# Attention score banks of a fused attention and mixture-of-experts kernel: two heads' third key blocks share a bank, and the loop's step is reordered

## What is computed

```
h = xn @ W1 + b1                       # q, k, v of 16 heads, d = 8
w = einsum(q, k) / sqrt(8), causal
a = softmax(w) @ v
attention = a @ Wp + bp
ffn(x) = (silu(x @ gate.T) * (x @ up.T)) @ down.T     # 352 hidden
routed = top-2 of 8 experts by softmax(xn @ gate_w.T), weights renormalised
out = x + attention + shared_ffn(xn) + routed(xn)
```

## Time and profile before

| | |
|---|---|
| Median of 3 runs | 563.29 us (558.61 to 565.58) |
| The profiled execution | 564.77 us |
| Its span, first to last instruction | 563.0 us |
| Mean granted TensorE clock | 0.931 |
| PE, DVE, ACT, POOL busy | 92%, 70%, 55%, 57% |
| Attention loop, about | 16.7 to 333 us of the span |

### The profile page before, as it was taken

How to read it: one execution, slowest core, us unless ns; L and a number is a source line. 1 busy time by engine, 2 the same in 40 slices (tenths; PEclk the granted TensorE clock), 3 DMA queues, 4 the chain that set the end, 5 groups by cost and what they waited for, 6 DMA issues and landing times.

```text
span 563.0 us, 13933 instructions
## 1 busy us (share of the span) xinstructions
PE 519.4 (92%) x4584; PEld 339.4 (60%) x4585; DVE 396.2 (70%) x753; ACT 310.1 (55%) x684; POOL 322.8 (57%) x382
## 2 busy tenths in 40 slices
PE   8879999989999899998988898999999999999995
PEld 3334445444454454444444247999999999977673
DVE  6895678886879878678777555555555555548896
ACT  2015878776777767687666653433333333355542
POOL 5449652342558768577777723676665544475442
PEclk9875999998989999799889669999999999999998
DMA  5424631130111435613111112221122222334555
GB/s 160 153 83 165 209 142 65 48 125 22 59 58 49 168 114 189 184 49 129 36 53 36 49 29 58 62 69 57 58 68 61 56 67 64 113 108 126 156 154 148
DMA packets 52156, 53.46 MB, mean 95 GB/s; under 512 B 5744, under 2 KB 39568, under 8 KB 51856
## 3 DMA queue, kind: packets, MB, share of 16 engines
q1 hardware_dynamic: 47616, 43.71, 24.6%
q0 software_dynamic: 4352, 8.95, 4.8%
q10 hardware_dynamic: 144, 0.20, 0.1%
HBM read 20.38 MB, written 17.90 MB: 68 GB/s over the span
## 4 chain that ended last, share of the span: by engine, by line
PE 68%; DVE 12%; ACT 8%; issue 6%; DMA 4%; DVEq 1%; POOL 1%; SPq 1%; ACTq 0%; POOLq 0%
PE av_bank L879 15%; PE av_bank L1052 9%; PE mx_pair L824 8%; DVE neg_max L1542 5%; PE st_banks L852 5%; ACT probs L1243 4%; PE st_banks L1063 4%; DVE o_sb L1718 3%; PE mx_pair L1038 2%; PE mx_pair L1042 2%; PE mx_pair L1041 2%; PE mx_pair L1043 2%; PE mx_pair L1039 2%; PE mx_pair L1040 2%; PE st_banks L1028 2%
## 5 line engine op out<-in xcount | busy, mean ns | idle before, releaser
L1542 DVE TENSOR_REDUCE neg_max<-mx_pair 128x2 f32<-128x256 f32 (+3 forms) x256 | 203.0, 822 | 64.6 <-PE mx_pair L835 61.9
L1243 ACT ACTIVATE probs<-st_banks 128x512 f32<-128x512 f32 (+1 forms) x384 | 181.3, 526 | 78.9 <-PE st_banks L852 76.6
L852 PE MATMUL st_banks<-q_st,k_st 32*128 32x128 f32 (+3 forms) x512 | 98.6, 414 | 18.2 <-ACT probs L1243 17.2
L705 POOL DMA_INDIRECT y_tok<-y_sb,y_rows x72 | 70.0, 972 | 76.1 <-ACT y_sb L1348 61.5
L824 PEld LDWEIGHTS mx_pair<-k_st,q_st 31*128 31x128 f32 x512 | 45.0, 193 | 96.4 <-DVE neg_max L1542 53.3
L879 PE MATMUL av_bank<-probs,v_wide 128*18 128x512 f32 (+3 forms) x1024 | 100.4, 491 | 0.0
L824 PE MATMUL mx_pair<-k_st,q_st 31*128 31x256 f32 (+3 forms) x512 | 91.7, 399 | 8.8 <-DVE neg_max L1542 8.5
L852 PEld LDWEIGHTS st_banks<-q_st,k_st 32*128 32x128 f32 x512 | 49.4, 193 | 36.1 <-ACT probs L1243 24.3
L629 POOL DMA_INDIRECT sorted_x<-xn_rows,slot_idx x64 | 63.5, 993 | 13.3 <-issue 12.7
L1341 ACT ACTIVATE sg<-mx_pair 128x352 f32<-128x352 f32 x72 | 33.4, 464 | 61.6 <-PE mx_pair L1043 61.6
L588 POOL TENSOR_SCALAR_AFFINE_SELECT probs<-probs 128x1024 f32<-128x1024 f32 x32 | 34.9, 1092 | 53.6 <-ACT probs L1243 53.6
(11 more groups left out here) (214 smaller groups left out, 897.9 us busy)
## 6 DMA issues: line engine op xcount, KB each, us to landing
sorted_x<-zeros SPq DMA_DIRECT2D x8, 580.5 KB, 4.2
xg<-sorted_x SPq DMA_DIRECT2D x36, 129.0 KB, 2.2
picked<-y_tok SPq DMA_DIRECT2D x16, 256.0 KB, 3.8
q_st<-q_hi SPq DMA_DIRECT2D x14, 256.0 KB, 2.5
k_st<-k_hi SPq DMA_DIRECT2D x14, 256.0 KB, 2.5
egu_lo<-in_e_gu SPq DMA_DIRECT2D x2, 1408.0 KB, 6.6
x_all<-in_x SPq DMA_DIRECT2D x8, 256.0 KB, 3.6
att_T<-a_T SPq DMA_DIRECT2D x8, 256.0 KB, 2.1
```

The lines of the kernel that those rows point to most:

```text
L705: pool.indirect_dma_start(y_tok, bass.IndirectOffsetOnAxis(ap=y_rows[:, t, k:k + 1], axis=0), y_sb[t % 2][:, k, :], None).then_inc(y_st[t ...
L852: ins = pe.matmul(st_banks[:, i % 3, lo:lo + w], k_st[buf][32 * j:32 * j + 32, g, kb * P:(kb + 1) * P], q_st[buf][32 * j:32 * j + 32, g, k ...
L1243: act.activation(dst, src, ACT.Exp, scale=SCALE).then_inc(st_free, 1)
L1542: ins = dve.tensor_reduce(neg_max[:, g, h:h + 2, qb], mx_pair[i % 2][:, :, lo:lo + (qb + 1) * P], AX.X, ALU.max, negate=True)
```

## The change

The third key blocks (block 2) of two heads now share one bank: unit 8 holds heads 0 and 1, unit 9 heads 2 and 3, 256 columns for each head. `third_scores(n, 0)` writes the left halves (heads 2 and 0) in visit 4, `third_scores(n, 1)` the right halves (heads 3 and 1) in visit 5, after a wait for the left ones (`third_half`). ACT takes both banks after visit 5, with two exponentials of 512 columns in place of four of 256. On PE, V3 moves to where V1 was, V1 to where V3 and V2 were, and V2 to between visit 4 and visit 5. The second misc work moves behind visit 5, and ACT copies it out after the exponentials of units 9 and 8. ACT's copy of `av_bank` moves behind the exponentials of heads 4, 5 and the first misc work. The new PE order is: visit 0 (S 2, 3), V0, visit 1 (S 0, 1), `m`, V3, visit 2 (S 6, 7), V1, visit 3 (S 4, 5), first misc, visit 4 (left halves), V2, visit 5 (right halves), second misc.

```
-ST_PARTS = [[(0, 0)], [(3, 0), (1, P)], [(2, 0)]]
+ST_PARTS = [[(0, 0)], [(3, 0), (1, P)]]
+THIRD = 8
...
-        scored = [("S", s, u) for u in (2, 3, 0, 1, 6, 7, 4, 5, 10, 11, 8, 9)] if s >= 0 else []
-        order += scored[0:4] + ([("m", s + 1)] if -1 <= s < GROUPS - 1 else []) + scored[4:8] + first_misc(s) + scored[8:10] + second_misc(s) + scored[10:12]
+        scored = [("S", s, u) for u in (2, 3, 0, 1, 6, 7, 4, 5, THIRD + 1, THIRD)] if s >= 0 else []
+        order += scored[0:4] + ([("m", s + 1)] if -1 <= s < GROUPS - 1 else []) + scored[4:8] + first_misc(s) + scored[8:10] + second_misc(s)
...
+            def third_scores(n, k):
+
+                b, g = divmod(n, NG)
+                buf = b % NBUF
+                w = S - 2 * P
+                if k == 1:
+                    pe.wait_ge(third_half, 2 * (n + 1))
+                for half in (1, 0):
+                    i, j = ST_NO["S", n, THIRD + half], 2 * half + k
+                    if k == 0:
+                        pe.wait_ge(st_free, i - 2)
+                    pe.matmul(st_banks[:, i % 3, k * w:(k + 1) * w], k_st[buf][32 * j:32 * j + 32, g, 2 * P:3 * P],
+                              q_st[buf][32 * j:32 * j + 32, g, 2 * P:S], start=True, stop=True,
+                              skip_group_check=True).then_inc((third_half, st_full)[k], 1)
...
-                if kb == 1:
+                if kb in (1, 3):
                     pe.wait_ge(masked, 3 * n + 2)
...
                 if valued:
-                    values(s - 1, 1)
+                    values(s - 1, 3)
                 if maxima:
                     max_scores(s + 2, 2)
...
                 if valued:
-                    values(s - 1, 3)
-                    values(s - 1, 2)
+                    values(s - 1, 1)
                 if maxima:
                     max_scores(s + 2, 3)
...
                 if scored:
-                    scores(s, (10, 11))
+                    third_scores(s, 0)
                 if maxima:
                     max_masks(s + 2, 4)
+                if valued:
+                    values(s - 1, 2)
+                if maxima:
+                    max_scores(s + 2, 5)
+                if scored:
+                    third_scores(s, 1)
+                if maxima:
+                    max_masks(s + 2, 5)
                 if s == -2:
                     x_transposes(1)
...
-                if maxima:
-                    max_scores(s + 2, 5)
-                if scored:
-                    scores(s, (8, 9))
-                if maxima:
-                    max_masks(s + 2, 5)
...
-                if s >= 1 and s % GP == 0:
-                    results_out_of(s - 1)
                 if scored:
                     exponents(s, (4, 5))
...
+                if s >= 1 and s % GP == 0:
+                    results_out_of(s - 1)
                 if scored:
-                    exponents(s, (10, 11))
+                    exponents(s, (THIRD + 1, THIRD))
...
-                if scored:
-                    exponents(s, (8, 9))
```

More of the change, by code:

```diff
@@ L56 @@
 NMX = 6
-ST_PARTS = [[(0, 0)], [(3, 0), (1, P)], [(2, 0)]]
-NST = 12
+ST_PARTS = [[(0, 0)], [(3, 0), (1, P)]]
+THIRD = 8
 PRIME_HID, PRIME_HIDT, PRIME_Y = 1, 2, 3
@@ L306, in attention_moe_kernel @@
         st_full, st_free, mx_full, mx_free = (sem(n) for n in ("st_full", "st_free", "mx_full", "mx_free"))
+        third_half = sem("third_half")
         mask_set, mask_ld = sem("mask_set"), sem("mask_ld")
@@ L592, in mask_third @@
                 diag = probs[n % 2][:, 8:10, :].rearrange("p u (h w) -> p (u h) w", h=2)[:, :, 0:P]
-                pool.wait_ge(st_free, used_up("S", n, 9))
+                pool.wait_ge(st_free, used_up("S", n, THIRD))
                 pool.affine_select(out=diag, in_=diag, compare_op=ALU.is_ge, fill=0.0, base=0,
@@ L1234, in exponents @@
                     act.wait_ge(st_full, i + 1)
-                    src, w = st_banks[:, i % 3, :], 2 * P
+                    src = st_banks[:, i % 3, :]
                     if u < 4:
                         dst = probs[n % 2][:, u, :]
-                    elif u < 8:
+                    elif u < THIRD:
                         dst, src = probs_by_block[n % 2][:, :, u - 4, :], src.rearrange("p (c w) -> p c w", w=P)
                     else:
-                        dst = probs[n % 2][:, 8 + (u - 8) // 2, u % 2 * w:(u % 2 + 1) * w]
-                        src = src[:, 0:w]
+                        dst = probs[n % 2][:, u, :]
                     act.activation(dst, src, ACT.Exp, scale=SCALE).then_inc(st_free, 1)
```

## The result

| | before | after |
|---|---|---|
| Median | 563.29 us (558.61 to 565.58) | 572.85 us (567.87 to 574.54) |
| Profiled execution, span, clock | 564.77, 563.0, 0.931 | 567.87, 566.1, 0.957 |
| Clock of the other executions | | 0.936 to 0.942 |

The changed kernel is slower, by 1.6%: ratio 1.0158, 95% interval 1.0116 to 1.02. Its profiled execution happens to be its fastest, with the highest clock, so the trace shows 3.1 us of the 9.6 us. In all ratios here, executions more than 1.5% above the fastest of their kernel are left out, so a ratio can be lower than the quotient of the medians.

The account below looks back on a forecast made before the run. No engine alone bounds it: PE, DVE and ACT wait in turn in visits 3 to 5, and the clock falls. Terms -9.5 - 1.2 + 0.9 - 1.3 = -11.1 us on 564.77 give 553.7; forecast 554 us, range 549 to 566.

Parts of the forecast that it names:

- odd steps: Worked on step 15: visit 2's scores start 0.25 us earlier, V2 and unit 9 give some back; -0.15 us.
- the sum: Step lengths over the loop: 13 even steps +0.2, 13 odd ones -0.13, together +0.9 us; bounds -5 and +14.
- Shared rows: Heads 0 and 3 use PE rows of their visit's maxima: at most 0.1 us on DVE's side, counted 0.
- The even step: Worked on step 16: the copy waits for V2, then unit 9 delays the next S 2, 3; +0.2 us.
- The falls: Clock drops to half speed, 3.4 us each, from 80 to 311 us: eight of nine gone, -9.5 us.
- the thin place: Visits 3 to 5 of a step without projection, where engines wait in turn; V2 there should end the falls.
- The first rival: The falls stay: PE's idle time is only spread, so the clock still falls; 563 us at the median, chance 0.30.
- the tail: From 311 to 336 us: one clock fall of five gone, -1.2 us.
- all falls go: Rival in which the tail's falls go too: 548 us, chance 0.12.
- The start: Step -2: x transposes behind visit 5 let DVE reduce without a gap; -1.3 us, bounds 0 and -1.3.
- The new wait and the queues: `third_half` before the right halves is already met, 0; SP's queue sees the same waits in the same order.
- ACT starves, slower: V2 ahead of the right halves delays both wide exponentials: up to +0.5 us a step, +14 us; chance 0.08.

Follow-up runs that it names:

- The square of the two parts: Old or shared banks with old or new value order, second misc behind visit 5 in all four: rounds 33.19, 33.09 (old banks), 33.14, 35.07 us (shared).
- free rows: Changed kernel with the shared banks' heads exchanged between visits 4 and 5, so third-key matmuls avoid PE rows of their visit's maxima: 558.77 us, ratio 0.989.
- the late misc: Kernel before with only the second misc work moved behind visit 5: 556.54 us, ratio 0.9885.
- the value order alone: Kernel before with only V3 before visit 2, V1 before visit 3, V2 behind visit 4 and the av_bank copy later: 555.76 us, ratio 0.9856.

## Why the prediction was wrong

**The step that failed** is the one on odd steps, "V3 in V1's place is 0.4 us shorter, so they start at 182.56 [...] **-0.15 us**". Measured, odd steps grew: 9.48 for 8.69 and 8.94 for 8.36, +0.8 and +0.6, and the steps from 4 to 27 together by 8.6 us at full clock, for which the sum had +0.9. Three things were wrong in it.

- *The scores of visit 2 start no earlier.* Visit 2 needs the buffer that DVE is reducing, and the turn takes a buffer of the same pair. V1 stood under that wait; its leaving wins nothing (2.91 for 2.93 us). I had taken PE as the limit in step 15 because it was busy, though some of its work stood where it would otherwise have waited.
- *V2 was hidden and now isn't.* "V2 and the full-width unit 9 give some of it back" sized as part of 0.25 what costs V2's whole 0.56 to 0.63 us. V2 behind visit 5 undid it: -2.1 us a round. The square of the two parts shows that it costs only with shared banks: with the old ones ACT has two exponentials to do under V2.
- *Shared rows.* "At most 0.1 us a visit, on DVE's side [...]: 0". It was 0.27 us between the two third-key matmuls of a visit, on the side of the scores and thus of unit 9's exponential, 0.85 us a round. I weighed who waits for the maxima and not who waits for the scores.

**The even step** came out nearly right in number, in part by luck. For a thin one I predicted +0.2 us (about 8.0) and it took 8.13, +0.3. But with free rows it takes 7.83, as before the change: the shared rows, which I had at 0, are worth the whole 0.3, and the rest of the step came out 0.2 us better than my working. The copy waits for V2 and the last pair follows it, as worked out. In a thin step ACT's row of step 16 has

```profile
197.70 0.60 ACT L1272 ACTIVATE av_sb<-av_bank 128x512 f32<-128x512 f32 x1 [0.75 <-PE av_bank L895]
198.21 1.08 ACT L1259 ACTIVATE probs<-st_banks 128x512 f32<-128x512 f32 x2
```

with the idle time inside the 0.3 to 0.9 that I named. Steps of kind 4n+2 won 0.2 through the late misc, which I had at 0; alone it is worth 0.44 a round.

**The falls.** I took eight of nine falls in 80 to 311 us as gone, 9.5 us. In the profiled execution 17 of the 31 us at half clock were left there; in the median one the clock was 0.942 for 0.934, 8 us less at half speed, some 3 us won. The term was mis-sized by two thirds, and its reason (V2 fills the thin place) is not borne out: the value order alone, with V2 there, does raise the clock to 0.958, but the kernel with free rows and V2 behind visit 5 leaves that place empty and has the highest clock of all (0.960), while exchanging V1 and V3 takes it back to 0.934. The first rival's mechanism came nearer. The Trainium skill (TensorE: Matmul & The Clock Gate, "A second HAM failure mode: psum-queue depth-cycling") says that short idle gaps between groups of matmuls make the clock oscillate; the clock here went down and up in every kernel whatever filled the thin place, which agrees as far as it goes, but the page doesn't say which gaps matter.

For the tail I took one fall of five as gone. In the profiled execution none of the 17 us at half clock is left from 311 to 336, and the loop's last values come 4.3 us sooner after the start of step 28 (at 333.5 for 334.4). But two falls of 3.4 us now begin at 336.0 and 342.8, in the first experts, whose first down projection starts 3.9 us later after those values (at 347.2 for 344.3). So three of five went, and the end of the loop as a whole won next to nothing. In the case "all falls go" the sum has 5 us for the tail that had been worked out as 6; it should give 547.

**The start.** The 1.3 us came out in number with the transposes moved alone (1.56 in the profiled execution, 1.8 of the median, interval 0.4 to 3.9), but its reason is shown only in part: the wait of 1.34 us was read at half speed, and at the old place without it the wait is 0.47. In the changed kernel step 0 was 1.18 us early, 0.93 of it from before step -2, and step 4 only 0.13: steps 0 to 3 used it up.

**The new wait and the queues** cost nothing that the rows show: PE's rows behind `third_half` follow without idle time.

**The rivals.** The one that came true is "ACT starves, slower", to which I gave 0.08. Its mechanism and place were right (ACT idle 1.13 us before the last pair), and +0.36 a step on average lies within its "up to +0.5", though 0.21 of that is the shared rows, which it hadn't counted. I set it aside because the even step, which I worked out in full, seemed to have room; it hadn't either, as it takes 7.54 us with V2 behind visit 5 and 8.13 with V2 ahead. By Perfetto Trace Analysis of the Trainium skill, "Optimizing Scalar/DVE Operations", where an engine isn't saturated but holds others up, smaller instructions may let work be done sooner. The traces agree for these exponentials once V2 stands ahead (34.22 us a round for wide on free rows, 33.09 for narrow), and not with V2 elsewhere (33.14 for wide, 33.19 for narrow).

## What to carry to other kernels

Work on the busiest engine was free here where that engine would have waited anyway. Before moving a block, find for both its old place and its new one what it hides under: here each of two places hid up to 0.85 us whichever block stood there, and the new one hid nothing. When two results are merged into one larger unit, everything ahead of the later half delays the use of both; so merging and putting work ahead of the later half should be tried apart and together, as here: with the late misc in all, the one alone was 1.9% faster, the other 2.9%, and the two together 1.6% slower, by the ratios. Work out the step kinds with the least slack in full, not the one that is easiest to follow.

## What the runs showed of the hardware

- Two matmuls on 32 rows each, of which one uses rows that a matmul beside it uses too, started 0.27 us apart (225.88 and 226.15); with all on rows of their own they started together (218.06, x2). The Trainium skill (TensorEngine Tiling (Array Packing), "Key Properties") says that different tiles of the array can work in parallel; the pair on free rows agrees. What shared rows cost here is 0.27 us for a matmul of 256 columns.
- The order of two blocks of value matmuls, with the same work and, at full clock, the same step lengths to 0.02 us, moved the mean granted clock from 0.960 to 0.934 and the median time by 12 us (7 by the ratios). The same exchange in the changed kernel took the clock from 0.942 to 0.935 and cost 6 us, of which the clock explains about 3. PE's busy share of the stretch before a fall (2.50 and 2.78 of 3.4 us, against 2.54 and 2.55 with no fall) doesn't tell them apart. Why is open.
- Where a fall of the clock lies changes what a wait seems to cost: DVE's wait for the x transposes and visit 5 in step -2 was 1.34 us with the clock at 0.5 from 25.0 us on, and 0.47 us in a kernel with the same order there whose clock fell behind most of that work.
